# Adding an attention result to the edge columns of a convolution's input with one operation per unit in place of eight

## What is computed

```python
h = cond(x, cond_128, ...)            # per batch: mixes the channels, adds a bias
q, k, v = h @ Wq, h @ Wk, h @ Wv      # q: 32 values x 32 heads; k, v: 32 values
o = sum_e softmax_e(q[d, h] * k[e] * scale) * v[e]
x = x + broadcast(o)                  # o[d] goes to the 32 positions 32 d .. 32 d + 31
c = conv1d(x, weight, taps 9, padding 4, groups 4) + context + bias
x = x + c @ dequantized(packed_weight).T + ffn_bias
```

## Time and profile before

| | us |
|---|---|
| median of 3 runs | 431.62 |
| lowest, highest | 431.26, 432.72 |
| the profiled execution | 432.14 |
| its span in the trace | 430.2 |
| TensorE busy | 412.6 (96%) |
| DVE busy | 363.5 (85%) |
| GpSimd busy | 340.9 (79%) |
| ScalarE busy | 226.8 (53%) |

### The profile page before, as it was taken

The page is one execution under the profiler, slowest core; times in us unless marked ns, Lnnn a source line. Parts: engine busy times, 40 slices in busy tenths (PEclk is TensorE's granted clock), DMA queues, the critical chain, the costliest instruction groups (busy, mean ns, idle before and its releaser), DMA issues.

```text
span 430.2 us, 6661 instructions
## 1 busy us (share of the span) xinstructions
PE 412.6 (96%) x2195; PEld 348.8 (81%) x2195; DVE 363.5 (85%) x603; ACT 226.8 (53%) x465; POOL 340.9 (79%) x316
## 2 busy tenths in 40 slices
PE   3969899899999999999999999999999999999997
PEld 2969799778888888888888888888888888888885
DVE  2896999998989899899989799998989799983421
ACT  3854655556455274657446365647264465562700
POOL 4033948769686999999999979899979979999920
PEclk9988999999999999999999999999999999999999
DMA  8989246470637565664736290928174371816112
GB/s 312 385 330 379 102 149 225 146 270 5 182 106 265 192 220 202 181 240 143 281 100 223 62 350 20 329 88 259 63 237 185 69 254 38 287 41 234 48 52 98
DMA packets 21752, 79.05 MB, mean 184 GB/s; under 512 B 5704, under 2 KB 5832, under 8 KB 17352
## 3 DMA queue, kind: packets, MB, share of 16 engines
q1 hardware_dynamic: 21416, 77.21, 51.2%
q10 hardware_dynamic: 288, 1.18, 0.9%
HBM read 61.11 MB, written 17.27 MB: 182 GB/s over the span
## 4 chain that ended last, share of the span: by engine, by line
PE 79%; DVE 6%; DMA 2%; issue 1%; POOL 1%; ACT 0%; DVEq 0%; POOLq 0%
PE p_f L1159 51%; PE p_conv L1153 19%; PE p_sm L1129 7%; PE p_sm L1138 1%; DMA o_c<-o_dram 1%; DMA o_dram<-o_sb 1%; DVE den L837 1%; DVE c_lo L882 1%; DVE xc L876 1%; DVE prob L828 1%; DVE prob L833 1%; DVE p_sm L845 1%; POOL xc L440 0%; DVE p_ut L893 0%; DVE prob L841 0%
## 5 line engine op out<-in xcount | busy, mean ns | idle before, releaser
L1159 PE MATMUL p_f<-w_ffn,u_hi 128*128 128x512 f32 x512 | 195.8, 392 | 0.0
L1159 PE MATMUL p_f<-w_ffn,u_lo 128*128 128x512 f32 x512 | 194.9, 390 | 0.0
L610 ACT ACTIVATE u_sb<-p_conv,u_bias,cols_sb 128x128 f32<-128x128 f32 x256 | 95.0, 460 | 42.2 <-PE p_conv L1153 40.2
L1159 PEld LDWEIGHTS p_f<-w_ffn,u_lo 128*128 128x128 f32 x512 | 96.2, 188 | 20.5
L1159 PEld LDWEIGHTS p_f<-w_ffn,u_hi 128*128 128x128 f32 x512 | 96.1, 188 | 20.5
L453 POOL TENSOR_TENSOR c_lo<-xc,c_hi 128x516 fp32r<-128x516 f32 (+1 forms) x66 | 82.7, 1263 | 11.6 <-ACT c_hi L600 6.8
L464 POOL TENSOR_TENSOR xn<-xn,bias_n 128x1024 f32<-128x1024 f32 x32 | 76.3, 2403 | 4.7 <-DMA xn<-xn_in_in 4.6
L600 ACT ACTIVATE c_hi<-xc 128x516 fp32r<-128x516 f32 (+1 forms) x68 | 41.0, 608 | 65.0 <-POOL xc L445 59.8
L440 POOL TENSOR_TENSOR xc<-xc,o_c 128x384 f32<-128x384 f32 x60 | 54.3, 905 | 24.5 <-DMA o_c<-o_dram 23.3
L906 DVE TENSOR_TENSOR xn<-p_f,xn 128x512 f32<-128x512 f32 x64 | 43.4, 678 | 23.8 <-PE p_f L1159 23.4
L893 DVE STREAM_TRANSPOSE p_ut<-u_sb 128x512 f32<-128x512 f32 (+1 forms) x68 | 45.8, 680 | 16.4 <-ACT u_sb L610 16.3
(11 more groups left out here) (113 smaller groups left out, 458.6 us busy)
## 6 DMA issues: line engine op xcount, KB each, us to landing
xc<-xc_in_in SPq DMA_DIRECT2D x16, 1032.0 KB, 8.8
xn<-xn_in_in SPq DMA_DIRECT2D x16, 1024.0 KB, 7.1
out<-xn SPq DMA_DIRECT2D x31, 512.0 KB, 7.0
xt<-xt_in_in SPq DMA_DIRECT2D x15, 1024.0 KB, 5.6
o_c<-o_dram SPq DMA_DIRECT2D x15, 256.0 KB
xn<-wq_in SPq DMA_DIRECT2D x4, 512.0 KB, 12.4
xt<-wq_in SPq DMA_DIRECT2D x1, 1024.0 KB, 6.8
xn<-wq_in SPq DMA_DIRECT2D x1, 1024.0 KB, 8.8
```

What stands on the lines that cost most here:

```text
L610: ins = eng.activation(u_sb[:, g % 2, i * P:(i + 1) * P], p_conv[g % 2][:, i * P:(i + 1) * P], ACT.Identity, bias=u_bias[:, g, bat:bat + 1 ...
L1159: return mm(p_f[half][:, :], u[:, (k // TU) % 2, r, t * P:(t + 1) * P], w_ffn[:, r, 512 * half:512 * half + 512], **flags)
```

## The change

`o` comes back twice. `o_sb` gets two more columns, which GpSimd sets to zero once, and `divide` writes between them; so each `o` row has a zero at either end. `save_o` still writes the 32 values to `o_dram`, and now also the 34 to a second array `o_pad`. `spread_o` still reads `o_c`, and then reads `o_pad` into `cw_o`, in one transfer for each half of the partitions, the second one a value further on. So the lower half sees 0, o0, ..., o31 and the upper half o0, ..., o31, 0, each of 33 values: one for each of the 33 edge columns. One operation of 128 partitions x 16 rows x 33 columns then adds them for the whole unit: `add_edges` on GpSimd ahead of the adds of steps 3 to 16, and on DVE for step 2. `add_o` keeps only the three-column operation, and does not wait between the groups. `cw_o` lies where the convolution's unsplit weights `cw` were, which are not needed after the start; the memory set aside for generated transfers is halved (`dynamic_dma_scratch_size`).

```diff
-        cw = sb("cw", [P, 2, G, P])
+        cw_o = sb("cw_o", [P, 2, UB * G, DH + 2])
...
+        o_pad = nc.dram_tensor("o_pad", [NU, CG * UB * G * (DH + 2)], F32).ap()
...
             def save_o(a, t):
                 eng.wait_ge(s_o, TU * a + t + 1)
+                eng.dma_start(o_pad[a].rearrange("(c k d) -> k c d", c=CG, k=UB * G)[t * TN * G:(t + 1) * TN * G, :, :], o_sb[:, a % 2, t, :]).then_inc(s_pw, 16)
...
             def spread_o(a):
                 eng.wait_ge(s_ow, 32 * a)
                 eng.wait_ge(s_add, added(max(a - 1, 1), G - 1))
+                if a == 3:
+                    eng.wait_ge(s_edge1, 1)
+                if a > 3:
+                    eng.wait_ge(s_edge, a - 3)
                 eng.dma_start(o_c[:, a % 2, :, :, :].rearrange("p n g d -> p (n g d)"),
...
+                eng.wait_ge(s_pw, 32 * a)
+                if a == 1:
+                    eng.wait_ge(s_cwl, 1)
+                for h in range(2):
+                    eng.dma_start(cw_o[64 * h:64 * h + 64, a % 2, :, :].rearrange("p k d -> p (k d)")[:, 0:RUN],
+                                  o_pad[a].rearrange("(c e) -> c e", c=CG)[:, h:h + RUN].unsqueeze(0).broadcast_to([R // 2, CG, RUN])).then_inc(s_oe[a % 2], 16)
...
+            def add_edges(p):
+                b = unit_of(p)
+                eng.wait_ge(s_xc[b % 2], 16 * (b // 2 + 1))
+                eng.wait_ge(s_oe[b % 2], 32 * ((b + 1) // 2))
+                c, o = edges(b)
+                eng.tensor_tensor(c, c, o, ALU.add).then_inc(s_edge, 1)
...
             def add_o(p, g):
...
-                eng.tensor_tensor(x4[0:64, :, :, 3], x4[0:64, :, :, 3], o[0:64], ALU.add).then_inc(s_add, 1)
-                eng.wait_ge(s_add, added(p, g) - 2)
-                eng.tensor_tensor(x0[64:P, :, :, 0], x0[64:P, :, :, 0], o[64:P], ALU.add).then_inc(s_add, 1)
...
             for p in range(5, NP):
+                add_edges(p)
                 add_o(p, 0)
...
             def add_edges():
 
                 eng.wait_ge(s_xc[1], 16)
-                eng.wait_ge(s_oc[1], 16)
-                for rows, at in ((slice(0, 64), 1), (slice(64, P), 0)):
-                    x = xc[rows, 1, :, :, at:at + P].rearrange("p n g (d j) -> p n g d j", j=4)[:, :, :, :, 3 * at]
-                    eng.tensor_tensor(x, x, o_c[rows, 1, :, :, :], ALU.add).then_inc(s_edge, 1)
+                eng.wait_ge(s_oe[1], 32)
+                c, o = edges(1)
+                eng.tensor_tensor(c, c, o, ALU.add).then_inc(s_edge1, 1)
```

More of the change, by code:

```diff
@@ L36 @@
 NP = NU + 1
+RUN = UB * G * (DH + 2) - 1
 AT = {}
@@ L80, in block_program @@
         rden = sb("rden", [P, TU, DH])
-        o_sb = sb("o_sb", [P, 2, TU, DH])
+        o_sb = sb("o_sb", [P, 2, TU, DH + 2])
         o_first = sb("o_first", [P, TU, P + 2])
@@ L88, in block_program @@
         w_ffn = sb("w_ffn", [P, R, D], F32R)
-        cw = sb("cw", [P, 2, G, P])
+        cw_o = sb("cw_o", [P, 2, UB * G, DH + 2])
+        cw = cw_o[:, :, :, :].rearrange("p s k d -> p (s k d)")[:, 0:2 * G * P].rearrange("p (k g o) -> p k g o", k=2, g=G)
         cw_hi = sb("cw_hi", [P, 2, G, P], F32R)
@@ L163, in o_val @@
                 return o_first[:, k, 1:P + 1].rearrange("p (d j) -> p d j", j=4)[:, :, 0]
-            return o_sb[:, (k // TU) % 2, k % TU, :]
+            return o_sb[:, (k // TU) % 2, k % TU, 1:DH + 1]
         def copies(p, g):
@@ L192, in block_program @@
         s_oz = sem("s_oz")
+        s_pw = sem("s_pw")
+        s_oe = [sem(f"s_oe{i}") for i in range(2)]
         s_sel = sem("s_sel")
@@ L234, in block_program @@
         s_edge = sem("s_edge")
+        s_edge1 = sem("s_edge1")
         s_ch = sem("s_ch")
@@ L266, in added @@
         def added(p, g):
-            return G * p + g + 1 if p <= TU else 3 * G + 3 * (G * (p - 3) + g + 1)
+            return G * p + g + 1
         def lowered(p, g):
@@ L276, in rows_of, with edges @@
             return v[:, n[0]:n[-1] + 1, g, :]
+        def edges(a):
+            c = xc[:, a % 2, :, :, :].rearrange("p n g m -> p (n g) m")[:, :, 0:MW:4]
+            return c.rearrange("p (n g) d -> p n g d", g=G), cw_o[:, a % 2, :, 0:DH + 1].rearrange("p (n g) d -> p n g d", g=G)
         def columns(v, p):
@@ L316, in save_o @@
                 eng.wait_ge(s_o, TU * a + t + 1)
-                eng.dma_start(o_dram[a, :, t * TN * G:(t + 1) * TN * G, :].rearrange("c k d -> k c d"), o_sb[:, a % 2, t, :]).then_inc(s_ow, 16)
+                eng.dma_start(o_dram[a, :, t * TN * G:(t + 1) * TN * G, :].rearrange("c k d -> k c d"), o_sb[:, a % 2, t, 1:DH + 1]).then_inc(s_ow, 16)
+                eng.dma_start(o_pad[a].rearrange("(c k d) -> k c d", c=CG, k=UB * G)[t * TN * G:(t + 1) * TN * G, :, :], o_sb[:, a % 2, t, :]).then_inc(s_pw, 16)
             def spread_o(a):
@@ L426, in _ @@
             eng.memset(o_first[:, :, :], 0.0).then_inc(s_oz, 1)
+            eng.memset(o_sb[:, :, :, :], 0.0).then_inc(s_oz, 1)
             eng.memset(mix_t[:, :, :, :], 0.0).then_inc(s_mixz, 1)
+            def add_edges(p):
[4 more added lines that the diff above has]
+                eng.tensor_tensor(c, c, o, ALU.add).then_inc(s_edge, 1)
             def add_o(p, g):
@@ L432, in add_o @@
                 x4 = xc[:, b % 2, :, g, 1:MW].rearrange("p n (d j) -> p n d j", j=4)
-                x0 = xc[:, b % 2, :, g, 0:P].rearrange("p n (d j) -> p n d j", j=4)
-                o = o_c[:, b % 2, :, g, :]
                 if g == 0:
@@ L437, in add_o @@
                     eng.wait_ge(s_oc[b % 2], 16 * ((b + 1) // 2))
[L438 to L442, removed]
-                eng.tensor_tensor(x4[0:64, :, :, 3], x4[0:64, :, :, 3], o[0:64], ALU.add).then_inc(s_add, 1)
-                eng.wait_ge(s_add, added(p, g) - 2)
-                eng.tensor_tensor(x0[64:P, :, :, 0], x0[64:P, :, :, 0], o[64:P], ALU.add).then_inc(s_add, 1)
+                eng.tensor_tensor(x4[:, :, :, 0:3], x4[:, :, :, 0:3],
+                                  o_c[:, b % 2, :, g, :].unsqueeze(3).broadcast_to([P, UB, DH, 3]), ALU.add).then_inc(s_add, 1)
             def c_low(p, g):
-                if p >= TU:
-                    eng.wait_ge(s_add, added(p, min(g + 1, G - 1)))
                 eng.wait_ge(s_ch, G * p + g + 1)
@@ L457, in x_bias @@
                 u = k // TU
-                if k % TU == 0 and u:
-                    eng.wait_ge(s_add, added(u + 1, G - 1))
                 eng.wait_ge(s_xn[u % NXN], 16 * (u // NXN + 1))
@@ L509, in _ @@
             c_low(2, 3)
+            add_edges(3)
             add_o(3, 0)
@@ L521, in _ @@
             x_o(5)
+            add_edges(4)
             add_o(4, 0)
@@ L596, in c_high @@
                 if p == TU and g == 0:
-                    eng.wait_ge(s_edge, 2)
+                    eng.wait_ge(s_edge1, 1)
+                if p > TU and g == 0:
+                    eng.wait_ge(s_edge, p - TU)
                 if p >= TU:
@@ L851, in divide @@
                 eng.wait_ge(s_rden, k + 1)
+                eng.wait_ge(s_oz, 2)
                 if a == 0:
-                    eng.wait_ge(s_oz, 1)
                     eng.tensor_tensor(o_first[:, t, 1:P + 1].rearrange("p (d j) -> p d j", j=4), num(0)[:, t, :].unsqueeze(2).broadcast_to([P, DH, 4]),
@@ L859, in divide @@
                     eng.wait_ge(s_ow, 32 * (a - 2))
+                    eng.wait_ge(s_pw, 32 * (a - 2))
                 eng.tensor_tensor(o_val(k), num(a)[:, t, :], rden[:, t, :], ALU.mult).then_inc(s_o, 1)
@@ L1458 @@
     }
-    nc = bacc.Bacc("TRN2", target_bir_lowering=False, num_devices=1)
+    nc = bacc.Bacc("TRN2", target_bir_lowering=False, num_devices=1, dynamic_dma_scratch_size=8192)
     args = {}
```

## The result

The changed kernel takes 447.1 us (median of 4 runs, 445.68 to 449.98), the kernel before 432.17 on the same chip: a ratio of 1.036 with a 95% interval of 1.033 to 1.038. It is **15 us slower**, far outside the predicted range of 429.9 to 433.3. The profiled execution is the one of 445.68 us; its span is 443.9 us, 13.7 more than before.

A forecast was written before the change was run, and what follows sets the result against it. TensorE was taken to bound the kernel after 94.64 us. Waits saved, -0.55 - 0.39 = -0.94 us, took the profiled 432.14 to 431.2; the run median lies 0.5 below, so 430.7 us, range 429.9 to 433.3.

The forecast's parts named there:

- What bounds the kernel: TensorE has no gap after 94.64 us; at most 1.18 + 0.39 = 1.57 us to gain at conv(2,1) and conv(3,0).
- GpSimd's relief: Edge operations on GpSimd: 59.0 us removed, 14 new ones of 1.4 us each added, GpSimd 39 us less busy.
- Step 2: DVE's single edge operation waits for `cw_o` at 67.6, ends at 68.6; DVE reaches c_low(2,1) at 73.8.
- rival 1: At c_low(2,1) GpSimd goes first again, DVE ends behind the second `x_bias`: +0.4 us, 432.0; chance 0.20.
- The likeliest course: DVE goes between the two `x_bias` at c_low(2,1); waits gone there and at conv(3,0): -0.94 us; chance 0.40.
- the landing of `cw_o`: Unit 2's last read lands 4.18 us after its issue, at 90.2, making the data 1.3 us later.
- my upper bound: Worst landing time for the `cw_o` reads: the 6.46 us that `o_c` of unit 1 took; data 3.6 us later.
- Rival 2: `cw_o` lands late and delays conv(3,0): +1.5 to +2.8 us, 433.1 to 434.4; chance 0.17.
- far half: The part of the late-landing rival's 433.1 to 434.4 us said to lie above the range's end of 433.3.
- What costs nothing: Steady part: SP's pads and second reads hold up loads by about 2.5 us, but those are wanted 20 us later.
- the room at the first group: Slack at a step's first group: 2.7 us at conv(4,0), 1.1 at conv(5,0), against data 1.3 to 1.9 us later.
- The last sentence of the prediction: Wrong if TensorE waits for GpSimd's `c_lo` while GpSimd waits for `cw_o`, at 94 us or any later step.

The follow-up runs named there:

- x_two: Kernel before, with two half-partition edge operations per unit from `o_c` in place of eight, ahead of the adds, no added transfer: 431.95 us, ratio 1.000.
- x_one_late_exp: Changed kernel with one `cw_o` read, edge operation behind the adds of groups 0 and 1, second `exp` ahead of `c_high`: 431.97 us, ratio 1.000.
- x_one_read: Changed kernel with `cw_o` read in one transfer for all 128 partitions, without the one-value shift: 434.5 us, ratio 1.008.
- x_late: Changed kernel with the edge operation behind the adds of groups 0 and 1 in place of ahead of them: 438.02 us, ratio 1.016.
- x_traffic: Changed kernel's transfers, but the kernel before's edge adds from `o_c`, nobody waiting for `cw_o` until the end: 432.06 us, ratio 1.003 against the kernel before.
- x_exp: Changed kernel with the second `exp` ahead of `c_high` of group 0 in ScalarE's loop from step 5 on: 438.68 us, ratio 1.017.
- x_late_exp: Changed kernel with the edge operation behind the adds of groups 0 and 1 and `exp` ahead of `c_high`: 435.75 us, ratio 1.008.

## Why the prediction was wrong

**What bounds the kernel: right.** It said that behind 94.64 us an engine which feeds TensorE can only lose, and that 1.57 us is all there is to gain. x_two (14.7 us less of GpSimd) and x_one_late_exp both come out at a ratio of 1.000. The 1.57 us itself was not put to the test: x_two still waits 0.91 us in step 2 and 0.97 us at conv(3,0), and no run is without these waits.

**GpSimd's relief: right** in size, -38.2 us for -39. The edge operation took 1.59 us for the 1.4 I took, between its bounds of 1.12 and 2.2; DVE's 1.12 us for the 0.7.

**Step 2: rival 1's course.** `cw_o` of unit 1 was there at 69.6 for 67.6 (bound 69.1). `o_pad` was seen landed only at 63.2, 5.2 us after its issue, for the 60.2 to 62.0 of the prediction. DVE's edge operation ended at 70.79, for the 68.6 of the prediction. DVE came to c_low(2,1) at 75.78, for 73.8 (bound 75.3), while the second `x_bias` ran, and ended just behind it, at 77.65; TensorE waited 1.8 us there, before 1.18. The likeliest course, in which DVE goes between the two, did not come about, and -0.94 us with it. Rival 1 priced that at +0.4 us, which would be a small thing.

**Where it failed: the landing of `cw_o`.** "The last lands 4.18 us after its issue, at 90.2, where `o_c` landed". The reads of unit 2 even went out earlier than I had them (the second at 84.6 for 86.0), and landed at 92.83, 8.2 us after that issue; my upper bound, 6.46 us, would have given 92.5. I priced the reads like `o_c`'s of before, and two things differ.

The first is how they are cut: two of 64 partitions with 4 phases, where `o_c` is one of 128 with 8. By x_one_read this is 1.6 us, the second issue included. The second I did not look at either, and by the runs it is the larger: their place in the order. Before, the read of `o_c` went out 3 us behind the 1 MB load of `xn`; now it goes out 0.6 us behind it and the `cw_o` reads behind both. In this order `o_c` alone takes 6.6 us (x_late) and a single `cw_o` read of unit 2 takes 7.2 (x_one_read, 82.89 to 90.11). The 4.18 us was the price of a read that met only the end of the load (share 0.97 from 84.0 to 86.2 us). At unit 3, where no load goes out just ahead, `o_c` takes 4.5 us (x_late, 111.32 to 115.85), as before, and the single `cw_o` read behind it still 6.3 (x_one_read, 110.73 to 117.03).

And I counted the mean share of 0.50 as a half that is free, but that is the mean of a stretch. From 86 to 87 us, while the `xn` load moves, the share is 1.02. From 88.7 to 89.8 us the engines stand mostly idle, and the `cw_o` reads do not get on faster for it; then the next loads move:

```profile
88.70:89.80 1.10, 1.10 (x7) 0.91 (x6) 1.10 (x2) 0.36 (x2) 0.00 (x0) 1.00 0.29 112
```

That the load is what holds `o_c` back is read from these shares and the order of the issues; no run moves the `xn` load alone. Rival 2 named the course, a padded copy that lands late and holds TensorE at conv(3,0), though not its cause, and had its first price right (+2.8 us, measured +2.9), with a chance of 0.17. The price is right in part by luck, since the reads went out earlier than it says and took longer than its bound.

**What rival 2 left out.** It ended at one wait: 433.1 to 434.4. (The range, up to 433.3, left out nearly all of that, not its "far half".) The wait is followed by 1.6 us of matmuls at the lower clock. And the paragraph "What costs nothing" was the larger error. What it says of the loads held up behind the pads is borne out by x_traffic. But it set the room at the first group, 2.7 us and 1.1 us, against data 1.3 to 1.9 us later, and knew of no later loss. The data were later by more, TensorE waited 0.77 us at 127.77 and 0.69 at 153.75, and then came the loop. What the text did not do was name what is queued behind the waiting instruction: GpSimd's edge operation waits, ScalarE's `c_high` waits for it, and behind that stands the `exp` on which the next unit's `o` depends. x_exp shows what this one place in ScalarE's list is worth: some 8 us. So two errors met: a landing time some 4 us short (8.2 us for 4.18), and a path through ScalarE that was not followed.

**The last sentence of the prediction** gave the right sign to look for: TensorE waits for GpSimd's `c_lo` with GpSimd itself waiting for `cw_o`, at 94 us and later.

## What to carry to other kernels

An engine that is relieved off the path gives nothing, but a wait put at the head of its list for that relief can put it on the path; price the transfer that it waits for by a transfer cut in the same way and issued as close behind the same loads, not by one of like size. Then ask of each engine that waits what stands behind the waiting instruction, and whether that feeds the next turn of the same transfer: if so, a delay does not stay in its unit but comes back in each. If a late operand can't be avoided, put work that doesn't need it ahead of it, on the waiting engine (x_late, 9 us) and on those that wait for that one (x_exp, 8 us).

## What the runs showed of the hardware

- A read with 8 phases in the source moved 186 to 195 GB/s at a share of 0.50 of the transfer engines (`o_c`, before and after); two such reads of 4 phases, in flight together, 87 to 112 GB/s at 0.26 to 0.29. Issuing halves side by side did not help.
- The same 256 KB read took 4.18 us to land when it went out 3 us behind a 1 MB load (before) and 6.6 us when it went out 0.6 us behind it (x_late).
- Behind a wait of TensorE of 3.08 us the granted clock was 0.56 over 3.9 us, and the matmuls started 0.43 us apart, not 0.23; behind 2.27 us at 202.37 it was 0.62 over 4.0 us, and behind 1.94 us (x_late_exp) 0.57 over 4.0 us. After one of 1.61 us (x_one_read) and one of 1.65 us (x_late) it stayed at 1.00 over 4 us, and the next matmuls took 0.39 us as ever.
- A 17 KB write was taken as landed 5.2 us after its issue for unit 1, and 2.1 to 2.4 us in the seven later units whose read waited for it; the prediction had 1.8 us for unit 1 and 3.57 for unit 2 (2.1 measured).
